# A graph attention layer with one-hot neighbours: when the last sums are read back, which waits guard the last strips, and how the final check crosses partitions

## The reference

```python
N, F_IN, F_OUT, H = (8192, 128, 128, 4)
h = jnp.maximum(_layernorm(x, axis=-1), 0.0)
proj = jnp.einsum('nf,hfo->hno', h, W)
s_src = jnp.einsum('hno,ho->hn', proj, a_src)
s_tgt = jnp.einsum('hno,ho->hn', proj, a_tgt)
scores = leaky_relu(s_src[:, :, None] + s_tgt[:, None, :], negative_slope=0.2)
attn = softmax(mask[None, :, :] + scores, axis=1)      # mask is adj, 8192 x 8192, over its rows i
vals = jnp.einsum('hij,hjo->hio', attn, proj)
vals = elu(vals + h[None, :, :])
out = x + vals.mean(axis=0)
```

## Time and profile before

| | us |
|---|---|
| median of 3 runs | 883.04 (883.02 to 883.87) |
| the profiled execution | 881.85 |
| its span | 880.0 |

### The profile page before, as it was taken

How to read it: one execution, slowest core, us unless ns; L and a number is a source line. 1 busy time by engine, 2 the same in 40 slices (tenths; PEclk the granted TensorE clock), 3 DMA queues, 4 the chain that set the end, 5 groups by cost and what they waited for, 6 DMA issues and landing times.

```text
span 880.0 us, 15010 instructions
## 1 busy us (share of the span) xinstructions
PE 695.0 (79%) x5016; PEld 586.6 (67%) x5016; DVE 788.3 (90%) x836; ACT 673.4 (77%) x1183; POOL 261.9 (30%) x163
## 2 busy tenths in 40 slices
PE   0292488897897898797978978978978888898994
PEld 0281478786786687686877877866967777884441
DVE  3797899899999999999999999999999897975997
ACT  0083397797797887977967977879789679897995
POOL 1000013214233332412331333223123221344996
PEclk9997699899899999999999999999899899999998
DMA  9999999999999999999999999999999999926913
GB/s 326 350 346 392 373 373 368 374 364 371 368 372 371 372 370 368 375 370 372 371 368 372 372 371 372 370 368 375 370 372 371 368 364 295 290 55 165 280 53 86
DMA packets 224012, 294.44 MB, mean 335 GB/s; under 512 B 4707, under 2 KB 218212, under 8 KB 223974
## 3 DMA queue, kind: packets, MB, share of 16 engines
q1 hardware_dynamic: 214226, 289.49, 95.8%
q0 software_dynamic: 9216, 4.20, 4.0%
q10 hardware_dynamic: 532, 0.27, 0.1%
HBM read 281.29 MB, written 12.65 MB: 334 GB/s over the span
## 4 chain that ended last, share of the span: by engine, by line
DMA 29%; DVE 28%; PE 20%; issue 13%; SPq 7%; ACT 3%; DVEq 0%; ACTq 0%; POOLq 0%
DMA arena<-in_adj 23%; PE ps L572 12%; DVE arena L768 11%; SPq L441 7%; DVE arena L793 6%; PE ps L538 5%; DMA sums<-arena 4%; DVE ps L798 3%; DVE arena L785 2%; ACT ps L683 2%; PE ps L621 2%; DVE arena L761 1%; DMA checked<-arena 1%; DVE arena L993 1%; DVE arena L959 1%
## 5 line engine op out<-in xcount | busy, mean ns | idle before, releaser
L683 ACT ACTIVATE ps<-ps,arena 128x1024 f32<-128x1024 f32 x512 | 559.3, 1121 | 159.2 <-PE ps L572 111.0
L572 PE MATMUL ps<-ident,arena 128*128 128x128 f32 x4096 | 538.0, 283 | 20.8 <-ACT ps L683 19.6
L572 PEld LDWEIGHTS ps<-ident,arena 128*128 128x128 f32 x4096 | 469.2, 146 | 76.1 <-ACT ps L683 71.7
L768 DVE TENSOR_TENSOR arena<-arena 128x3072 f32<-128x3072 f32 (+1 forms) x120 | 360.1, 3001 | 13.7 <-DMA arena<-in_adj 9.3
L502 POOL DMA_INDIRECT sums<-arena x64 | 161.1, 2517 | 529.1 <-DVE arena L835 288.8
L538 PE MATMUL ps<-ident,arena 128*128 128x128 f32 x512 | 81.1, 310 | 144.1 <-DVE arena L785 132.4
L538 PEld LDWEIGHTS ps<-ident,arena 128*128 128x128 f32 x512 | 66.5, 161 | 155.3 <-DVE arena L785 79.1
L683 ACT ACTIVATION_READ_ACCUMULATOR ps<-ps,arena 128x1 f32 x512 | 123.0, 240 | 0.0
L793 DVE TENSOR_REDUCE arena<-ps 128x1 f32<-128x1024 f32 x64 | 78.2, 1222 | 21.9 <-PE ps L538 21.4
L785 DVE TENSOR_TENSOR arena<-arena 128x1024 f32<-128x1024 f32 x64 | 76.5, 1221 | 7.4 <-DMA arena<-in_adj 6.8
L798 DVE SCALAR_TENSOR_TENSOR ps<-ps,arena 128x1024 f32<-128x1024 f32 x64 | 82.1, 1282 | 0.0
(11 more groups left out here) (89 smaller groups left out, 241.4 us busy)
## 6 DMA issues: line engine op xcount, KB each, us to landing
arena<-in_adj SPq DMA_DIRECT2D x160, 1536.0 KB, 14.9
arena<-in_adj SPq DMA_DIRECT2D x8, 1024.0 KB, 10.3
arena<-in_adj SPq DMA_DIRECT2D x16, 512.0 KB, 7.4
sums<-arena SPq DMA_DIRECT2D x1, 4160.0 KB, 23.7
out<-arena SPq DMA_DIRECT2D x15, 256.0 KB, 2.7
arena<-sums SPq DMA_DIRECT2D x6, 512.0 KB, 7.9
sums<-arena POOLq DMA_INDIRECT x64, 7.3
arena<-sums SPq DMA_DIRECT2D x4, 256.0 KB, 3.1
```

The source lines that it names most:

```text
L572: mm = pe.transpose(turned_ps[buffer_of(g, i, n)][:, m, :], piece(g, i, r)[:, m, q * P:(q + 1) * P], ident[:, :])
L683: act.activation(turned, turned, ACT.Exp, scale=KAPPA, bias=cert[:, i, q, G:G + 1], accum_out=cert[:, i, q, r:r + 1]).then_inc(f_exp, 1)
L768: dve.tensor_tensor(acc_of(g, i), acc_of(g, i), piece(g, i, r), ALU.max).then_inc(f_acc, 1)
```

## The change

1. `added_before` waits for the adds up to the strip before the former one (two strips back instead of one), and only from strip 3 on.
2. In strip 19 `find_target(18)` stands right behind `find_same(18)`, ahead of `piece_max` 2 of strip 20.
3. SyncE reads the first 8 tiles when the first chunk of set 63 is turned and set 61 is added (before: all chunks turned, set 62 added). GpSimd holds the add of set 62 until they have landed. VectorE marks set 62's targets as well (`mark_ahead`, two operations in strip 23); TensorE multiplies them (`sums_ahead`) and adds the loaded tiles, both before `open_banks`, and adds set 63 on top with `last_sums`, the first of them ahead of `sum_same`.
4. `turn_sums(2)` moves from ahead of pair 2 to behind it; the stages of blocks 0, 1 and 2 move with it.
5. `bad` is turned by TensorE into PSUM behind project 28, and `set_flag` reads that behind pair 29. The store and load of `checked` go.

```diff
     def added_before(engine, g, i):
-        if not known(g) or number(g, i) > 1:
-            engine.wait_ge(f_added, sets_to(*former_of(g, i)) * 16)
+        if not known(g) or number(g, i) > 2:
+            engine.wait_ge(f_added, sets_to(*former_of(*former_of(g, i))) * 16)
...
-    CHECKED = 9
-    FLAG_AT = 26
+    TURN_FLAG_AT = 28
+    FLAG_AT = 29
...
-            sp.wait_ge(f_turn, NT * G)
-            sp.wait_ge(f_added, (NT - 1) * 16)
+            sp.wait_ge(f_turn, (NT - 1) * G + 1)
+            sp.wait_ge(f_added, (NT - 2) * 16)
             for k, (t0, t1) in enumerate(SUMS):
                 if k == EARLY:
+                    sp.wait_ge(f_turn, NT * G)
                     sp.wait_ge(f_added, NT * 16)
...
-                if k == CHECKED:
-                    sp.wait_ge(g_d, CHECKS - 2)
-                    sp.dma_start(checked.rearrange("(p k) -> p k", k=1), bad[:, 0:1]).then_inc(g_b, 16)
-                    sp.wait_ge(g_b, 16)
-                    sp.dma_start(bad_row, checked.rearrange("(k p) -> k p", k=1)).then_inc(g_r, 16)
...
-                    if last_strip(g, i):
+                    if known(g) and Q == STRIPS - 2:
                         for k in range(EARLY):
                             pool.wait_ge(t_agg[k], 16)
...
+            def sums_ahead(k):
+                pe.wait_ge(t_ahead, k + 1)
+                pe.wait_ge(f_h, NT - 1)
+                pe.matmul(agg_ps[k % 2], h[:, NT - 2, 0:F], hot_ahead[:, k * QUAD * P:(k + 1) * QUAD * P], start=True, stop=True)
...
+            def turn_check():
+                pe.wait_ge(g_d, CHECKS - 2)
+                pe.wait_ge(t_stage, NT // QUAD - 1)
+                pe.transpose(bad_ps, bad[:, 0:1].to_broadcast([P, P]), ident[:, :]).then_inc(g_r, 1)
...
             strips_of(pe, strip)
+            pe.wait_ge(f_exp, NT * G + BUFFERS - 2)
+            for k in range(EARLY):
+                sums_ahead(k)
+            for k in range(EARLY):
+                add_sums(k)
             pe.wait_ge(f_exp, NT * G + BUFFERS - 1)
             open_banks(0)
             pe.wait_ge(f_exp, NT * G + BUFFERS)
             open_banks(1)
             turn_idx((STRIPS - 1) // BODY, (STRIPS - 1) % BODY)
+            last_sums(0)
             sum_same((STRIPS - 1) // BODY, (STRIPS - 1) % BODY)
-            last_sums(0)
-            add_sums(0)
+            last_sums(1)
             pe.wait_ge(f_rows, STRIPS)
             open_banks(2)
-            last_sums(1)
             pe.wait_ge(t_part, 1)
             project(0)
-            add_sums(1)
             project(1)
-            turn_sums(2)
             for k in range(1, NT // QUAD):
                 for w in range(k * QUAD // 2, (k + 1) * QUAD // 2):
                     project(w)
+                    if w == 2:
+                        turn_sums(2)
+                    if w == TURN_FLAG_AT:
+                        turn_check()
...
                     find_same(*before)
+                    dve.wait_ge(t_at, 1)
+                    dve.wait_ge(f_idx, STRIPS - 1)
+                    for k in range(EARLY):
+                        mark_ahead(k)
                     find_target(*before)
...
                 if soon:
+                    find_target(*before)
                     piece_max(*after, 2)
                 piece_max(*after, 3)
                 piece_max(*after, 4)
                 piece_max(*after, 5)
-                if not first_strip(g, i):
+                if not first_strip(g, i) and not soon:
                     find_target(*before)
                 piece_max(*after, 6)
...
+            def mark_ahead(k):
+                cols = slice(k * QUAD * P, (k + 1) * QUAD * P)
+                dve.tensor_scalar(hot_ahead[:, cols], row_at[:, cols], idx[:, (STRIPS - 2) % BODY, 0:1], None,
+                                  ALU.is_equal).then_inc(t_ahead, 1)
...
-                dve.wait_ge(g_r, 16)
-                dve.tensor_reduce(flag_f[0:1, 0:1], bad_row, AX.X, ALU.max).then_inc(g_d, 1)
+                dve.wait_ge(g_r, 1)
+                dve.tensor_reduce(flag_f[0:1, 0:1], bad_ps[0:1, :], AX.X, ALU.max).then_inc(g_d, 1)
...
+            stage_sums(0)
             find_target((STRIPS - 1) // BODY, (STRIPS - 1) % BODY)
-            stage_sums(0)
+            stage_sums(1)
             check_rows()
-            stage_sums(1)
             for w in range(PAIRS - 1):
                 elu(w)
-                if w % 2 == 1 and w * 2 // QUAD + 2 < NT // QUAD:
+                if w == 2:
+                    stage_sums(2)
+                if w % 2 == 1 and 2 < w * 2 // QUAD + 2 < NT // QUAD:
                     stage_sums(w * 2 // QUAD + 2)
```

More of the change, by code:

```diff
@@ L127, in peaked_path @@
     sums_t = sums.rearrange("(t p) f -> p t f", p=P)
-    checked = nc.dram_tensor("checked", [P], F32).ap()
     sums_rows = sums.rearrange("(p t) f -> p (t f)", p=P)
@@ L153, in peaked_path @@
     rows = A.take([BODY, NQ, F1])
-    bad_row = same[0:1, 0, :]
     zero = rows.rearrange("p i q f -> p (i q f)")[:, 0:ZERO]
@@ L191, in peaked_path @@
     hot = ring[:, 3, 2 * RT * P:2 * RT * P + EARLY_TILES * P]
+    hot_ahead = ring[:, 1, 2 * RT * P:2 * RT * P + EARLY_TILES * P]
     assert EARLY_TILES * P <= RT * P
@@ L201, in peaked_path @@
     m_last = v_ps[(PAIRS - 3) % 3][:, :, 0:2, :]
+    bad_ps = agg_ps[0][:, 0:P]
     s2_last = agg_ps[1][:, 0:2 * O].rearrange("p (t o) -> p t o", t=2)
@@ L247, in peaked_path @@
     t_hot = sem("last_targets_marked")
+    t_ahead = sem("targets_ahead_of_last_marked")
     t_turn = sem("tail_sums_turned")
@@ L266, in peaked_path @@
     g_m = sem("check_largest_norm")
-    g_b = sem("check_stored")
-    g_r = sem("check_row_landed")
+    g_r = sem("check_vector_turned")
     d_begin = sem("peaked_path_done")
@@ L592, in strip, with add_sums @@
                         turn_maxima(*latter_of(g, i), 0)
+            def add_sums(k):
+                pe.wait_ge(t_agg[k], 16)
+                for u in range(QUAD):
+                    pe.matmul(agg_ps[k % 2][:, u * P:(u + 1) * P], agg[:, k * QUAD + u, :], ident[:, :], start=False, stop=True,
+                              skip_group_check=True)
+            def sums_ahead(k):
+                pe.wait_ge(t_ahead, k + 1)
+                pe.wait_ge(f_h, NT - 1)
+                pe.matmul(agg_ps[k % 2], h[:, NT - 2, 0:F], hot_ahead[:, k * QUAD * P:(k + 1) * QUAD * P], start=True, stop=True)
             def last_sums(k):
@@ L597, in last_sums @@
                 pe.wait_ge(f_h, NT)
[L598 to L606, removed]
+                pe.matmul(agg_ps[k % 2], h[:, NT - 1, 0:F], hot[:, k * QUAD * P:(k + 1) * QUAD * P], start=False, stop=True,
+                          skip_group_check=True).then_inc(t_turn, 1)
             def turn_sums(k):
@@ L1059, in _ @@
             find_rows((STRIPS - 1) // BODY, (STRIPS - 1) % BODY)
-            dve.wait_ge(t_at, 1)
             dve.wait_ge(f_idx, STRIPS)
```

## The result

| | before | after |
|---|---|---|
| median, 7 runs each, us | 883.04 (881.87 to 883.87) | 887.12 (885.42 to 888.05) |
| ratio, 95% interval | | 1.0048 [1.0037, 1.0059] |
| span of the profiled execution, us | 880.0 | 885.4 |

What follows compares the result with a forecast made beforehand. Bound by VectorE (744 to 780 us), ScalarE (780 to 795), then a fixed pace with all three engines full, a serial chain between. 881.85 - 1.6 + 1.45 = 881.7; median 1.19 higher: 882.9 us, range 880.7 to 885.2.

Steps and rivals of the forecast that it cites:

- the flag: Last pairs: VectorE's 1.50 us wait in `set_flag` goes; -1.6 us, bounds -1.0 to -2.2.
- the head: Tail start: early tiles delay `turn_idx` on TensorE, `turn_sums(4)` waits for tiles 16 to 23; +1.45 us, bounds 0 to +2.86.
- The pace: Tail pairs: they run at one fixed pace, so lateness at the first pairs stays to the end; no term of its own.
- the flag rival: At `set_flag`: the wait only changes form, VectorE and GpSimd lock each other, only 0.6 us back: 883.9 us; chance 0.08.
- Strip 19: `find_target(18)` waits for ScalarE's copy, VectorE idles some 5 us, the later maximum starts 1.26 us later.
- The looser row wait: ScalarE's copy of strip 21's sums loses its 0.73 us wait, but chunk 7 still waits on TensorE: no gain.
- The slower rival: Tail start: the early tile loads land after TensorE wants them; over 884.8 us; chance 0.18.
- The rule on marks and descriptor writing: Strip 23: VectorE's two new marks lock GpSimd out of descriptor writing; set 61 lands some 0.8 us later, adding nothing.

Runs made afterwards that it cites:

- the flag kernel: The kernel before with only the check vector turned by TensorE and the flag set behind pair 29, no store and load: 883.07 us, ratio 1.0007.
- the kernel with the gap filled: The kernel before with eight more unused transposes on TensorE before the first bank is opened: 881.39 us against 882.39, ratio 0.9993.

## Why the prediction was wrong

Forecast: -1.6 for the flag, +1.45 for the head, pace unchanged, sum -0.15. Measured in the two traces: -0.42, +2.59, +2.05, sum +4.2.

- **The pace (failed).** "Pairs run through at one fixed pace, so whatever is late at the first pairs stays late to the end" left out that this pace rests on how VectorE's two-input operations fall against GpSimd's additions. Rows 1 showed VectorE and GpSimd full together, 25.96 and 25.05 of 26 us, and one-element operations of 0.68 us with two inputs stood in the timeline beside others of 0.14 us with one. The prediction named the mutual lock in the flag rival only, at 0.6 us and as a loss of gain. As a term it was worth 2.05 us, half of the result. The runs with scalar operations show it.
- **The flag (sized wrong).** The exps gained 1.74 us, as read from TensorE's and GpSimd's waits. The end gained 0.42, since VectorE ends last and its work isn't less; `set_flag` moved to where that counts. And 1.50 us of wait in one execution was the highest of five (0.17 to 1.50); in the other four the old flag costs less at the end than the new one.
- **Strip 19 (right, size too, in the traces).** Idle 4.91 us for "some 5", the next maximum at 744.96 for 744.94 forecast. At `find_rows(23)` +1.44 for +1.26; the rest is within what other traces vary by (-0.31 to +0.58 where this part is absent).
- **The looser row wait (right as far as seen).** No wait in the copy, and chunk 7's exp waits for TensorE instead. No run has this edit by itself.
- **The head (right mechanism, sized low).** Without the 1.22, `turn_idx` started at 799.13 for 798.85, `sum_same` at 800.10 for 799.84, the last add 3.10 us later for 2.86. The reload of tiles 16 to 23 took 8.96 us instead of 8.1, so `turn_sums(4)` was 2.60 late for 1.45. It was a wait within the stated bounds of 0 to 2.86; the experiment with the tiles ahead of x removes it.
- **Rivals.** None described what happened. The slower rival (early tiles awaited) is refuted: `add_sums` at 797.70 follows the products with no wait. The rule on marks and descriptor writing wasn't put to the test, since the marks started at 790.27, after set 61's add had been issued (787.80, 1.58 us). The row that was read as fitting it, the add at 781.45 with 2.40 us, has another neighbour on VectorE, a maximum with two inputs in SBUF:

```profile
781.17 1.22 DVE L785 TENSOR_TENSOR arena<-arena 128x1024 f32<-128x1024 f32 x1
```

  It ends at 782.39 and the add 1.46 us later. In the trace of the kernel before, 44 of the 64 adds start during such a maximum (L761, L768, L785), and every one of them ends 1.42 to 1.61 us behind it; the other 20 take 1.54 to 1.58 us. (In the changed kernel 3 of 45 don't follow.) So this was the wait of the check operations the other way round, and the trace that the forecast was made from showed it.
- **The range.** Its bounds came from the known terms; the missing term lay outside. The forecast also rested on one trace of the kernel before, in which the clock didn't fall (below) and the wait at the flag was unusually long.

## What to carry to other kernels

When VectorE and GpSimd are both full, read the short operations: a one-element operation of 0.68 us beside others of 0.14 us was waiting for the other engine here, and an edit upstream that shifted the phase made it 1.22 us. Writing it with one tensor input and a per-partition scalar took the wait away. A wait read from one trace can be an unusual one: look at the same wait in more traces before it goes into a sum. Work put "into a gap" of an in-order queue has to be counted against the instruction behind the gap that the critical chain needs, on every queue that the new work touches.

## What the runs showed of the hardware

TensorE's clock can fall after the short lull between the strips and the tail. Stretches of the flag kernel, of the kernel before and of the kernel with the gap filled, in this order (columns as in rows 1):

```profile
792.00:797.00 5.00, 2.77 (x15) 1.22 (x13) 1.00 (x5) 5.00 (x10) 0.80 (x1) 1.00 0.35 72
797.00:801.00 4.00, 3.62 (x11) 2.58 (x12) 1.24 (x6) 1.58 (x3) 1.19 (x1) 0.57 0.19 58
```

```profile
792.00:797.00 5.00, 2.39 (x14) 0.98 (x12) 1.41 (x7) 4.88 (x9) 0.61 (x1) 1.00 0.41 92
797.00:801.00 4.00, 4.00 (x18) 2.61 (x19) 2.50 (x9) 2.41 (x3) 1.54 (x1) 1.00 0.11 32
```

```profile
792.00:797.00 5.00, 3.68 (x22) 2.08 (x21) 0.97 (x5) 5.00 (x11) 0.83 (x1) 1.00 0.35 76
797.00:801.00 4.00, 3.59 (x17) 2.44 (x18) 2.55 (x8) 2.49 (x4) 1.46 (x1) 1.00 0.18 53
```

In the flag kernel the granted clock from 797 to 801 us was 0.57 on average (0.50, the 1.2 GHz level, for about 3 us) where the kernel before had 1.00, after much the same idle time. Its product for set 63 took 1.91 us instead of 1.02; the first exp came 1.7 us later, counted from `find_rows(23)`, and from pair 2 on the exps were 1.0 us later. The kernel with strip 18's targets sooner, which has the same head, fell in the same way. So it fell in two of the three traces with the bare gap, and in none of the thirteen with work in it. By these traces the old start costs about 1 us in some executions, and the profiled execution of the kernel before didn't show it. What decides between the two isn't shown here, and no run's time settles whether filling the gap pays.
